# A two-layer decoder on one core: first item, phase seams and last products put in another order

## The reference

```
x = x + L0_attn(layernorm(x))         # per item, 16 heads of 16
x = x + L0_xattn(layernorm(x), ctx)   # per item, keys and values from ctx
x = x + L0_ffn(layernorm(x))          # 16 experts, top 1, 512 places each
x = x + L1_attn(layernorm(x))         # attention over the 32 items, per token
x = x + L1_xattn(layernorm(x), ctx)   # per item, keys and values from ctx
x = x + L1_ffn(layernorm(x))          # per item, 4-bit blocks of 16

# L0_attn: sines from a table of 1024, causal
theta = x / (1 + |w|) + b;  i = round(theta * 1024 / 2 pi) mod 1024
Q = [cos_q, sin_q];  K = [cos_k, sin_k];  V = x @ v_w.T
out = softmax(causal(Q K^T / sqrt(32))) V @ out_w.T

# L0_ffn: a token's expert is the argmax; its place is the count of earlier
# tokens of that expert; past place 511 it is dropped (contributes 0)
y = relu(x W1[e] + b1[e]) W2[e] + b2[e];  out = y * max(softmax(x Wg + bg))

# L1_attn
out = softmax(tanh((x Wq^T)(x Wk^T)^T / 16)) x

# L1_ffn: q() quantises blocks of 16 to the grid 0, .5, 1, 1.5, 2, 3, 4, 6
out = q(silu(q(x) q(w_gate)^T) * (q(x) q(w_up)^T)) q(w_down)^T
```

## Time and profile before

| what | us |
|---|---|
| median of three runs | 3263.06 |
| lowest, highest | 3256.36, 3264.64 |
| profiled execution, whole | 3267.37 |
| its span | 3265.6 |
| PE busy | 3047.0 (93%) |
| DVE, ACT, POOL busy | 2325.0, 1779.8, 1275.3 |
| mean granted clock of PE | 0.97 |

### The profile page before, as it was taken

The page is one execution under the profiler, slowest core; times in us unless marked ns, Lnnn a source line. Parts: engine busy times, 40 slices in busy tenths (PEclk is TensorE's granted clock), DMA queues, the critical chain, the costliest instruction groups (busy, mean ns, idle before and its releaser), DMA issues. The chain is left out here.

```text
span 3265.6 us, 57391 instructions
## 1 busy us (share of the span) xinstructions
PE 3047.0 (93%) x21110; PEld 2129.6 (65%) x21110; DVE 2325.0 (71%) x4822; ACT 1779.8 (55%) x3245; POOL 1275.3 (39%) x1930
## 2 busy tenths in 40 slices
PE   5899999999999997699999796899999999999998
PEld 3576676776677764466666453577777777777775
DVE  4689989889999886142111584788887888887876
ACT  5688888888888873111111232554555554555553
POOL 5466666666666652000000451233333333333321
PEclk7999999999999997899999897999999999999999
DMA  7777887778877772432333354344333344333330
GB/s 149 139 107 115 114 119 104 111 113 113 113 116 103 109 93 37 158 113 94 116 121 113 97 168 88 51 64 70 64 59 58 58 67 70 63 60 58 58 50 14
DMA packets 290968, 301.17 MB, mean 92 GB/s; under 512 B 35110, under 2 KB 278294, under 8 KB 290688
## 3 DMA queue, kind: packets, MB, share of 16 engines
q1 hardware_dynamic: 276288, 273.43, 48.2%
q0 software_dynamic: 6144, 15.68, 2.0%
q10 hardware_dynamic: 8256, 8.39, 0.8%
HBM read 95.53 MB, written 50.40 MB: 45 GB/s over the span
## 5 line engine op out<-in xcount | busy, mean ns | idle before, releaser
L518 DVE TENSOR_REDUCE xa_mx<-bank 128x2 f32<-128x512 f32 x1024 | 662.4, 685 | 232.2 <-PE bank L508 222.5
L622 ACT ACTIVATE xa_p<-bank 128x512 f32<-128x512 f32 x1024 | 565.6, 596 | 300.9 <-PE bank L612 300.2
L633 DVE SCALAR_TENSOR_TENSOR xa_p<-xa_p,bank 128x1024 f32<-128x1024 f32 x256 | 303.6, 1217 | 93.2 <-ACT xa_p L622 74.9
L645 PE MATMUL bank<-xa_p,xa_v 128*32 128x256 f32 x4096 | 278.6, 390 | 1.4 <-DVE xa_p L633 0.9
L2016 POOL DMA_INDIRECT sa_y<-expert_out,sa_s x64 | 68.6, 1071 | 529.7 <-POOLq L1911 483.3
L959 ACT ACTIVATE xa_p<-bank 128x384 f32<-128x384 f32 x512 | 229.9, 503 | 59.7 <-PE bank L947 33.3
L968 POOL TENSOR_SCALAR_AFFINE_SELECT xa_p<-xa_p 128x256 f32<-128x256 f32 x512 | 209.1, 434 | 131.9 <-ACT xa_p L959 131.8
L1805 ACT ACTIVATE ex_h<-bank,ex_b 128x512 f32<-128x512 f32 x64 | 44.0, 687 | 362.1 <-PE bank L1794 362.1
L1794 PE MATMUL bank<-ex_xt,ex_w 128*128 128x512 f32 x512 | 225.0, 598 | 0.7 <-ACT ex_xt L1785 0.7
L1824 PE MATMUL bank<-ex_w,ex_h 128*128 128x256 f32 x1024 | 224.0, 379 | 1.0 <-issue 0.9
L508 PE MATMUL bank<-xa_ks,xa_qs 96*128 96x256 bf16 x1024 | 198.5, 277 | 22.6 <-DVE xa_p L633 10.6
(11 more groups left out here) (287 smaller groups left out, 6882.5 us busy)
## 6 DMA issues: line engine op xcount, KB each, us to landing
ex_w<-ra_parts SPq DMA_DIRECT2D x384, 128.0 KB, 4.7
xa_ks<-xa_pk SPq DMA_DIRECT2D x384, 128.0 KB, 5.3
ex_w<-in_L_ffn_W SPq DMA_DIRECT2D x32, 1024.0 KB, 7.3
xa_qs<-xa_pq SPq DMA_DIRECT2D x192, 128.0 KB, 4.7
ex_w<-xa_pq SPq DMA_DIRECT2D x192, 128.0 KB, 4.6
ra_x<-in_x SPq DMA_DIRECT2D x32, 256.0 KB, 7.8
xa_ctx<-in_ctx_t SPq DMA_DIRECT2D x64, 128.0 KB, 5.0
queue<-zeros ACTq DMA_DIRECT2D x4, 2048.0 KB, 12.8
```

The costliest lines, as they stand in the source:

```text
L518: c.nc.vector.tensor_reduce(c.xa.row_max[:, :, n], halves(c.banks[2 + n % 2]), AX.X, ALU.max).then_inc(s.max_taken, 1)
L622: c.nc.scalar.activation(c.xa.p_beside[:, n // 2 % 4, :, n % 2, :], halves(c.banks[n % 2]), ACT.Exp, scale=SCALE).then_inc(s.exp, 1)
L633: c.nc.vector.scalar_tensor_tensor(out=p, in0=p, scalar=1.0, in1=c.banks[bank][:, :].unsqueeze(1).broadcast_to([P, TC, 2 * S]), op0=ALU.mi ...
L645: m = c.nc.tensor.matmul(bank[WIDE * quad:WIDE * quad + WIDE, at + q0:at + S], v[:, kc, 4 * g + quad, :], p(4 * g + quad, kc), start=(kc = ...
```

## The change

At the start, the cast of the identity goes from POOL to ACT; POOL's second batch of constants waits until item 0 is normed; POOL's second power stands ahead of the low parts, and DVE's second norming ahead of the two memsets of `xa_ks`; item 0's stacking DMAs are issued as eight of high parts and then four of low parts, behind the loads of items 1 and 2. At the end of phase A, the last item's router norming is done by DVE; in every item POOL computes `keep`, `slots` and `gates` behind the indirect DMAs. Phase A's barrier stands in phase C behind SP's load of expert 0's rows. The eleven groups of turned matrices stand behind the last expert, and phase C has no barrier at its end: POOL, which gathers next, waits for the stores of the answers, and two PSUM banks keep their release. In phase D the first step adds and measures row by row, and POOL takes the first power ahead of the second gather. Phase D's barrier stands in phase E, behind the first two context loads and rows loads. At the very end the order is turn, down, turn, down.

```diff
+    k.cast = c.sem("ident_cast")
+    nc.scalar.activation(k.ident_bf[:, :], k.ident[:, :], ACT.Copy).then_inc(k.cast, 1)
...
+    c.pool.wait_ge(c.ra.s.ln, 4)
     for v in (*c.ra.v, *c.xa.v):
         c.step(c.pool_made, pool.memset(v[:, :, :, :], 0.0))
     c.step(c.pool_made, pool.memset(k.ones[:, :], 1.0))
     c.step(c.pool_made, pool.memset(k.ones_bf[:, :], 1.0))
-    c.step(c.pool_made, pool.tensor_copy(k.ident_bf[:, :], k.ident[:, :]))
...
+def sp_ra_first_stacks(c):
+    s, r = c.ra.s, c.ra
+    c.sp.wait_ge(s.high, 1)
+    for low in range(2):
+        for which, (stack, moved) in enumerate(((r.q_stack, s.q_in), (r.k_stack, s.k_in))):
+            if low:
+                c.sp.wait_ge(s.low, 2 * which + 2)
+            for n, slot in enumerate(SLOTS2):
+                if slot[which] == low:
+                    for kind in range(2):
+                        at = (2 * n + kind) * DH
+                        c.nc.sync.dma_start(stack[0][at:at + DH, :, :], r.parts[:, kind, slot[which], which]).then_inc(moved[0], 16)
...
+def dve_rt_last_normed(c):
+    b = B - 1
+    c.dve.wait_ge(c.rt.s.pow, b + 1)
+    s, r, x, dve = c.rt.s, c.rt, c.ra.x2[b % 2], c.nc.vector
+    c.dve.wait_ge(s.pow, b + 1)
+    c.dve.wait_ge(s.turned, b - 2)
+    c.dve.wait_ge(s.rows_out[b % 3], 32 * (b // 3))
+    for k in range(TC):
+        m = dve.tensor_scalar(r.xn[b % 3][:, k, :], x[:, k, :], r.mv[:, k, 0:1], r.rstd[:, k:k + 1], ALU.subtract, ALU.mult)
...
 def pool_rt_place(c, b):
-    columns = slice(TC * b, TC * b + TC)
     pool.tensor_scalar(r.base[:, :], r.rank[:, :], -float(CAP), float(E * CAP - 1), ALU.mult, ALU.add).then_inc(s.placed, 1)
     pool.tensor_scalar(r.over[:, :], r.place[:, :], float(CAP), FAR, ALU.is_gt, ALU.mult).then_inc(s.placed, 1)
     pool.tensor_scalar(r.at[:, :], r.place[:, :], float(CAP), None, ALU.min).then_inc(s.placed, 1)
-    pool.tensor_scalar(r.keep[:, :], r.place[:, :], float(CAP), None, ALU.is_le).then_inc(s.placed, 1)
+    c.pool.wait_ge(s.placed, at + 5)
+    pool.tensor_tensor(r.over[:, :], r.over[:, :], r.at[:, :], ALU.add).then_inc(s.placed, 1)
-    pool.tensor_tensor(r.over[:, :], r.over[:, :], r.at[:, :], ALU.add).then_inc(s.placed, 1)
-    pool.tensor_tensor(r.slots[:, columns], r.base[:, :], r.at[:, :], ALU.add).then_inc(s.placed, 1)
-    pool.tensor_tensor(r.gates[:, columns], r.gate[:, :], r.keep[:, :], ALU.mult).then_inc(s.placed, 1)
-    c.pool.wait_ge(s.placed, at + 9)
-    c.pool.wait_ge(s.placed, at + 10)
+    c.pool.wait_ge(s.placed, at + 7)
     c.pool.wait_ge(s.rows_out[b % 3], 32 * (b // 3))
     pool.tensor_copy(r.index[b % 3][:, :], r.over[:, :]).then_inc(s.placed, 1)
 def pool_rt_rows(c, queue, b):
-    s, r, at = c.rt.s, c.rt, b % 3
+    s, r, pool, at = c.rt.s, c.rt, c.nc.gpsimd, b % 3
+    columns = slice(TC * b, TC * b + TC)
-    c.pool.wait_ge(s.placed, 11 * b + 11)
+    c.pool.wait_ge(s.placed, 11 * b + 8)
     for k in range(TC):
-        c.nc.gpsimd.indirect_dma_start(
+        pool.indirect_dma_start(
+    pool.tensor_scalar(r.keep[:, :], r.place[:, :], float(CAP), None, ALU.is_le).then_inc(s.placed, 1)
+    pool.tensor_tensor(r.slots[:, columns], r.base[:, :], r.at[:, :], ALU.add).then_inc(s.placed, 1)
+    c.pool.wait_ge(s.placed, 11 * b + 9)
+    pool.tensor_tensor(r.gates[:, columns], r.gate[:, :], r.keep[:, :], ALU.mult).then_inc(s.placed, 1)
...
+    pool_ra_power(c, 1)
     dve_more_constants(c)
+    dve_ra_normed(c, 1)
+    dve_stack_rows(c)
...
+    for b in (1, 2):
+        sp_ra_load(c, x_rows[b], b)
+    sp_ra_first_stacks(c)
...
@@ phase_a
     router_stores(c, d)
-    c.nc.all_engine_barrier()
...
@@ pe_phase_c
-        if 4 <= e < 4 + TURNS:
-            pe_weights(c, e - 4)
         for q in range(QC):
             pe_c_down(c, e, q)
+    for n in range(TURNS):
+        pe_weights(c, n)
...
@@ act_phase_c
-            act_weights(c, e - 4)
+    for n in range(TURNS):
+        act_weights(c, n)
...
@@ phase_c
     setup_c(c)
+    sp_c_x(c, d["queue"].rearrange("(e c p) d -> e p c d", e=E, p=P)[0], 0)
+    c.nc.all_engine_barrier()
     raw_weights(c)
     sp_phase_c(c, d)
     pe_phase_c(c)
     act_phase_c(c)
     dve_phase_c(c)
-    c.nc.all_engine_barrier()
+    for out in c.ex.s.y_out:
+        c.pool.wait_ge(out, 16 * (E // 2))
...
@@ pool_d_gather
-            bounds_check=answer.shape[0] - 1, oob_is_err=False).then_inc(s.y_in[par], 16)
+            bounds_check=answer.shape[0] - 1, oob_is_err=False).then_inc(s.y_in[par] if t else s.y_first[g], 16)
...
+def dve_d_first(c):
+    s, r, dve = c.sa.s, c.sa, c.nc.vector
+    c.dve.wait_ge(s.x_in[0], 48)
+    for g in range(G):
+        c.dve.wait_ge(s.y_first[g], 16)
+        m = dve.scalar_tensor_tensor(out=r.x3[0][:, g, :], in0=r.y[0][:, g, :], scalar=r.gate[0][:, g:g + 1],
+                                     in1=r.x[0][:, g, :], op0=ALU.mult, op1=ALU.add)
+        done = (s.x3_first, g + 1) if g < G - 1 else (s.x3, 1)
+        m.then_inc(done[0], 1)
+        c.dve.wait_ge(*done)
+        m = dve.bn_stats(r.stats[:, g, :], r.x3[0][:, g, :])
+    m.then_inc(s.ln, 1)
+    dve_d_moments(c, 0)
...
@@ pool_phase_d
+    pool_d_gather(c, d["expert_out"], 0)
+    pool_d_power(c, 0)
     period = ROUND_D["pool"]
     for n in range((STEPS_D - 1) * period + 6):
-        for b, _ in due(n, period, (2,), STEPS_D):
+        for b, _ in due(n, period, (2,), STEPS_D, first=1):
             pool_d_gather(c, d["expert_out"], b)
-        for b, _ in due(n, period, (5,), STEPS_D):
+        for b, _ in due(n, period, (5,), STEPS_D, first=1):
...
@@ sp_phase_d
+    for b in range(2):
+        sp_xa_context(c, d["ctx_t"][b], B + b)
     for par in range(2):
         c.sp.wait_ge(c.sa.s.out_there[par], 16 * (STEPS_D // 2))
...
@@ pe_phase_e
 for tc in range(TC):
         pe_e_last_turn(c, tc)
-    for tc in range(TC):
         pe_e_last_down(c, tc)
...
@@ phase_e
     cross_tiles(c, 1)
     setup_feed_forward(c)
+    for b in range(2):
+        sp_e_load(c, d["x4"].rearrange("b (c p) d -> b p c d", p=P)[b], b)
+    c.nc.all_engine_barrier()
+    c.step(c.dve_made, c.nc.vector.memset(c.ff.hid_t[WIDTHS[-1]:P, FC - 1, :], 0.0))
+    c.pe.wait_ge(*c.all_of(c.dve_made))
     pe_phase_e(c)
     dve_phase_e(c)
```

70 lines of the change are left out of this document (38 added, 32 removed).

## The result

| | before | after |
|---|---|---|
| median, us | 3260.62 (4 runs) | 3238.52 (4 runs) |
| lowest, highest | 3256.36, 3264.64 | 3237.40, 3240.41 |
| profiled execution, its span | 3267.37, 3265.6 | 3238.66, 3236.8 |
| PE busy | 3047.0 | 3042.1 |

The ratio is 0.9933, with a 95% interval of 0.9916 to 0.9950: 22.1 us less (16 to 27 by that interval). The forecast was 3240.0 in a range of 3230 to 3252, and 23.0 us less. It counted from 3263.06, the median of the first three runs; from the 3260.62 of all four, 23.0 less is 3237.6. The profiled executions, though, lie 28.7 apart, so something in them is not the change.

The account below looks back on a forecast made before the run. The prediction saw steady matmul work, with PE busy 93% of the span, plus six seams priced alone. Terms 5.8 + 3.1 + 9.0 + 0.2 + 1.3 + 3.6 = 23.0 took 3263.06 to 3240.0 us, range 3230 to 3252.

Parts of the forecast that it names:

- Start, 5.8: Kernel start up to the first exp: reordered memsets, table load and stacking DMAs bring it 5.8 us earlier (4.4 to 6.5).
- the second chain: At the start, the second item's norming and sines, which ACT does before the first exp: exp 5.0 to 6.5 us earlier.
- The first chain: At the start, norming, high parts, stacking DMAs, first score matmul: matmul at 34.0 instead of 40.48, a gain of 6.45 us.
- First phase to experts, 3.1: Last router norming to PE's first expert turn: DVE norming, later small operations, no barrier before rows; 3.1 us (2.0 to 6.1).
- Experts, 9.0: Expert loop: eleven periods lose the turned matrices, which the gap behind expert 15 covers; 9.0 us gained (8.4 to 9.5).
- Batch attention, 0.2 (−0.6 to 2.4): Experts to batch attention: first turn gains 2.4 us, nearly eaten by the wait for the later second gather; 0.2 taken.
- Second cross attention, 1.3 (0.9 to 1.8): Second cross attention's start: context loads skip stores and barrier, the item's rows are asked for 1.35 earlier; 1.3 us gained.
- Very end, 3.6: Kernel end: twelve down matmuls fill PE's 2.91 wait and avoid the slow clock; 3.6 us gained, high end 3.9.
- (c): Every item: small operations behind indirect DMAs hold up POOL; the gain is spent from delay x = 2.84 us; chance 3%.
- (d): Experts: turns leave but the eleven periods stay at 29.49 us, say from loads; 14.0 less gain, 3249; chance 5%.
- (b): Seams: shorter gaps let PE keep its clock; 1.9 us back at three seams, 5.7 more gain, 3234.3; chance 12%.
- (a): Seams swallow each other: start 4.4, first phase's end 2.0, batch attention −0.6, end 1.5; 3245.5 us; chance 20%.

Follow-up runs that it names:

- the run on them: The changed kernel with keep, slots and gates ahead of the indirect DMAs and not behind: median 3236.72 us, ratio to the kernel before 0.9920.
- the second profile of before: The kernel before, with no edit, run and profiled again: median 3261.93 us (11 runs), ratio 1.0003.

## Why the prediction was right, and where it was not

- *Start, 5.8.* Measured 5.6, inside the 5.0 to 6.5 that I had for the second chain, and it is this chain that both kernels follow. The first chain's number, the matmul at 34.0, came out by errors that cancel. The 0.8 that I added for the rounding did not come (11.16 from the norming's end to the high parts, 11.22 without it), and the stacks no longer set the matmul: from the first stacking DMA to it were 16.1, not 15.3. Of the parts, the norming beside memsets is shown (4.84 against 0.84, worth 1.9 at the first exp); the order of second norming and memsets and the table load's 1.28 were not tried alone.
- *First phase to experts, 3.1.* Measured 3.6 to 3.8. The mechanism held: slots and gates are what SP waits for, as the term had it (the expectation of the run on them forgot that). What it did not ask is whether moving them paid: with them ahead the seam gains 1.2 more, which two runs showed. And the high end of 6.1 was out of reach, since PE also waits for the barrier, which POOL's drain holds until 19.1 to 19.2 behind the last power: from the 24.2 to 24.4 of before, that leaves a gain of at most 5.0.
- *Experts, 9.0.* Measured 8.9, and 8.95 by undoing it (the rows' own sum, 324.37 less eleven times 28.68, is 8.9). The gap hid them, as said.
- *Batch attention, 0.2 (−0.6 to 2.4).* Measured 1.6 to 2.7, so this term was mis-sized. The step that failed is the row landing time: I took 9.34 from the second gather's last issue to the norming; it was 7.75 (1810.74 to 1818.49). In the new order the rows were added 2.85 after that issue, the 1.5 that I had kept for the other end, and the second turn came 0.8 earlier. I also read the gain off at the second turn, but ACT's exp stood ahead of the next copies before, and that gave 0.7 more. The rest, up to the last sum, lies within what two executions of the same kernel differ (1.1). That the second norming holds the second turn is right for the changed kernel (PE waits 0.88 for it), but with the gather back ahead the turn came later and not earlier.
- *Second cross attention, 1.3 (0.9 to 1.8).* Measured 0.6 to 0.7, below its range. The context loads did leave the path: the projection waited for the barrier instead, and still ended 0.1 ahead of the turn. The step that failed is that the item's own rows are asked for 1.35 earlier. They were asked for only 0.5 sooner behind the last sum (4.29 against 4.82), since the last store landed 0.7 to 0.8 later than in the kernel before (4.2 to 4.3 behind the last sum, not 3.5). With a landing at 3.5 the 1.35 would have been right. The context loads, now under way beside the store, fit as the cause in every profile that shows the landing; a run of the changed kernel with no context load ahead was not made.
- *Very end, 3.6.* Measured 3.9 and 2.3 against the two profiles of before. The price of the slow clock was the uncertain part: the 24 matmuls took 7.67 in the first profile and 6.10 in the second, and in the changed kernel with the old order at its end 6.85. The step that was mis-sized is this price: I had taken it from the one profile at hand, which is the dearest of the three with the old order; the other two put the term at 2.3 and 2.6.

**The old order at the end**, whose run belongs here:

```diff
         pe_e_last_turn(c, tc)
+    for tc in range(TC):
         pe_e_last_down(c, tc)
```

> The changed kernel with turn, turn, down, down at its very end. Theory: 3.9 us back, 3242.4: the second turn waits 2.9 with PE idle and the 24 down matmuls take 7.7, half of them at the slow clock. Rival: the clock has nothing to do with it, the 24 take 5.5 and only 1.7 come back.

Median 3239.76 (5 runs), ratio 0.9934 (0.9921 to 0.9948). From the first last turn to the last add it is 11.50 against 8.86: 2.6, between theory (3.9) and rival (1.7), with the clock costing half of what I had said.

Of the rivals, (c) is refuted by the 1.93 and by the page's sum: the delay x is about 0.17 where 2.84 was needed. (d) is refuted by 28.67. (b) did not happen: PE still idled 6.75, 8.11 and 6.28 us ahead of the three stages, and the turn of expert 0, the first projection of the batch attention and that of the cross attention took 1.97, 5.78 and 3.78, against 1.97, 5.19 and 3.75 before. (That PE idled for over ten microseconds in each seam of the kernel before was misread: it was 7.02 at the cross attention and 2.91 at the end.) (a) did not happen either: none of its four seams came out at its low end, and the one below its range, the second cross attention, is one that (a) had left as taken. That the sum came out (23.0 against 22.1) owes something to errors of opposite sign: +0.5 or more at the first phase's end, +1.4 or more at the batch attention, −0.6 at the cross attention, −1.3 at the end by the second profile of before.

## What to carry to other kernels

Side work moved from a bound engine's loop into a gap that some other chain sets was worth its price to a tenth of a microsecond here, and the loop's own undisturbed period told that price beforehand. A wait removed at a seam is worth the distance to the next chain, so write down both chains and every engine that serves them (here ACT's copies, and POOL's drain ahead of a barrier). A time that agrees with the forecast does not show that its chain is the one that ends last: look for the idle time ahead of it. And judge an edit of a few microseconds between two places that bound it, in more than one profile: whole times here scatter by more than most of the terms.
